# A first router's scores made for both halves ahead of its choice, with two experts' products moved in between

## The reference, cut to what matters

```
def _L1_ffn_ref(x, gate_w, gate_b, w1, w2, w3):        # x: (16, 256, 64), as tokens: 4096 x 64
    logits = einsum('bsd,de->bse', x, gate_w) + gate_b # 16 logits a token
    probs = softmax(logits); top_probs, top_idx = top_k(probs, 2)
    top_probs = top_probs / sum(top_probs)
    dispatch = sum(one_hot(top_idx, 16) * top_probs[..., None], axis=-2)
    h1 = einsum('bsd,edh->bseh', x, w1)                # hidden 128
    h2 = einsum('bsd,edh->bseh', x, w2)
    expert_out = einsum('bseh,eho->bseo', silu(h1) * h2, w3)
    return einsum('bseo,bse->bso', expert_out, dispatch)
t = t + _L1_ffn_ref(_ln_t(t), ...)
```

## Time and profile before

| | us |
|---|---|
| median of 3 runs | 706.9 |
| the three runs | 706.47, 706.9, 711.89 |
| profiled execution, its own time | 704.68 |
| its span | 702.9 |
| TensorE busy in it | 623.2 (89%) |
| VectorE busy | 450.8 (64%) |
| ScalarE busy | 364.4 (52%) |
| GpSimd busy | 260.5 (37%) |

### The profile page before, as it was taken

The page is one execution under the profiler, slowest core; times in us unless marked ns, Lnnn a source line. Parts: engine busy times, 40 slices in busy tenths (PEclk is TensorE's granted clock), DMA queues, the critical chain, the costliest instruction groups (busy, mean ns, idle before and its releaser), DMA issues.

```text
span 702.9 us, 12272 instructions
## 1 busy us (share of the span) xinstructions
PE 623.2 (89%) x3776; PEld 412.3 (59%) x3776; DVE 450.8 (64%) x1323; ACT 364.4 (52%) x777; POOL 260.5 (37%) x349
## 2 busy tenths in 40 slices
PE   7887788886999999999998998998999999996784
PEld 5675437774555555555556776895545445465652
DVE  6555797878777787778776477565433333438566
ACT  3234586176544444444436454455666777435375
POOL 6402555250653543444353000270333333335153
PEclk8999998798999999999999899989999999999897
DMA  4900000204343433524301000022222222100001
GB/s 110 159 6 1 2 0 1 61 2 101 87 112 76 97 83 68 113 61 112 68 9 30 1 2 0 1 51 52 77 70 80 60 61 61 31 2 0 2 2 60
DMA packets 24532, 34.62 MB, mean 49 GB/s; under 512 B 10984, under 2 KB 20224, under 8 KB 22368
## 3 DMA queue, kind: packets, MB, share of 16 engines
q1 hardware_dynamic: 24480, 33.95, 20.8%
HBM read 32.50 MB, written 1.44 MB: 48 GB/s over the span
## 4 chain that ended last, share of the span: by engine, by line
PE 61%; DVE 24%; ACT 6%; issue 4%; POOL 3%; DMA 1%; DVEq 1%; ACTq 0%; SPq 0%; POOLq 0%
PE ps L1808 13%; PE ps L2384 9%; PE ps L2400 8%; PE ps L1828 6%; DVE ST L492 3%; PE ps L2506 2%; PE ps L426 2%; PE ps L784 2%; PE ps L609 1%; PE ps L2782 1%; PE ps L1589 1%; PE ps L2111 1%; PE ps L2089 1%; PE ps L2113 1%; DVE tk L1106 1%
## 5 line engine op out<-in xcount | busy, mean ns | idle before, releaser
L1500 POOL TENSOR_TENSOR out_acc<-out_acc,tok_tmp 128x512 f32<-128x512 f32 x80 | 103.6, 1295 | 211.3 <-DVE tok_tmp L1717 114.7
L1808 PE MATMUL ps<-tokT,w 128*128 128x512 f32 x512 | 134.5, 409 | 3.4 <-DVE hid_buf L1712 1.9
L1769 ACT ACTIVATE act_buf<-ps 128x512 f32<-128x512 f32 x128 | 75.8, 596 | 92.0 <-PE ps L1808 88.4
L1808 PEld LDWEIGHTS ps<-tokT,w 128*128 128x128 f32 x512 | 92.6, 190 | 52.6 <-issue 24.3
L2384 PE MATMUL ps<-tokT,w 128*128 128x512 f32 x256 | 67.7, 406 | 1.5 <-ACT hid_buf L2357 1.5
L2384 PEld LDWEIGHTS ps<-tokT,w 128*128 128x128 f32 x256 | 45.4, 188 | 28.4 <-ACT hid_buf L2357 13.9
L426 PE MATMUL ps<-ones 128*128 128x128 f32 x416 | 58.4, 294 | 1.4 <-DVE X L1005 1.4
L1712 DVE TENSOR_TENSOR hid_buf<-act_buf,ps 128x512 f32<-128x512 f32 x64 | 43.5, 685 | 19.9 <-ACT act_buf L1769 16.3
L426 PEld LDWEIGHTS ps<-ones 128*128 128x128 f32 x416 | 53.6, 206 | 3.9 <-DVE X L1005 1.7
L1712 DVE TENSOR_TENSOR tok_split<-act_buf,ps 128x512 f32<-128x512 f32 x64 | 43.4, 686 | 15.7 <-ACT act_buf L1769 14.7
L537 ACT ACTIVATE U<-X,nmr,rstd 128x64 f32<-128x64 f32 x104 | 36.5, 430 | 23.4 <-POOL nmr L515 18.3
(11 more groups left out here) (475 smaller groups left out, 1133.7 us busy)
## 6 DMA issues: line engine op xcount, KB each, us to landing
disp_all<-disp_dram SPq DMA_DIRECT2D x32, 512.0 KB, 6.1
disp_all<-disp_dram SPq DMA_DIRECT2D x32, 256.0 KB, 3.9
w_raw<-in_L_ffn_w SPq DMA_DIRECT2D x4, 512.0 KB, 7.8
XIN<-in_x SPq DMA_DIRECT2D x4, 256.0 KB, 3.8
w_raw<-in_L_ffn_W SPq DMA_DIRECT2D x2, 512.0 KB, 5.8
out<-XIN SPq DMA_DIRECT2D x4, 256.0 KB, 2.2
fc_raw<-in_L_conv_upfc_w SPq DMA_DIRECT2D x1, 512.0 KB, 4.6
w<-in_L_ffn_w SPq DMA_DIRECT2D x1, 512.0 KB, 11.6
```

Of the source, the lines that this page charges most:

```text
L1500: pool.tensor_tensor(out_acc[:, :], out_acc[:, :], weighed[p % 2], ALU.add).then_inc(mm["acc"].sem, 1)
L1769: act.activation(act_buf[e % 2][:, :], ps[:, e % 2, :], ACT.Silu).then_inc(mm["act"].sem, 1)
L1808: last = pe.matmul(ps[:, 2 * k + e % 2, :], w12[:, part, k, EXPERT1[e], :], tokT[:, bass.ts(i, CHUNK)], start=(part == 0), stop=(part == 1))
```

## The change

Four places move; no instruction is added or taken out, and no tile changes. VectorE makes the logits of both halves first, then five steps of the first half's choice, then the gate products of experts 0 and 1 of chunk 0, then the other six steps. The steps of the second half's choice, one behind each gate product, start at expert 2 in place of expert 0. TensorE makes `hidden(0, 2)` and `hidden(0, 3)` too ahead of the router's transposes of the first half. ScalarE moves their result behind the Silu of expert 3, not of expert 1.

```diff
             router_logits(dve, mm, route1, 0, E1, b_gw[:, :], 6)
+            router_logits(dve, mm, route1, 1, E1, b_gw[:, :], 7)
             for step in range(5):
-                router_top2(dve, mm, route1, 0, E1, step)
-            router_logits(dve, mm, route1, 1, E1, b_gw[:, :], 7)
-            for step in range(5, TOP2_STEPS):
                 router_top2(dve, mm, route1, 0, E1, step)
...
-                    if prev is None:
-                        router_top2(dve, mm, route1, 1, E1, e)
+                    if prev is None and e == 1:
+                        for step in range(5, TOP2_STEPS):
+                            router_top2(dve, mm, route1, 0, E1, step)
+                    if prev is None and e >= 2:
+                        router_top2(dve, mm, route1, 1, E1, e - 2)
...
-                    if prev is None and e == 1:
+                    if prev is None and e == 3:
                         router_move(act, mm, 0, 5)
...
-            router_transpose(pe, mm, route1, 0, (5, 6))
             wwait(pe, "w3")
...
                     if prev is not None or e >= 2:
                         hidden(i, e)
+                    if e == 3 and prev is None:
+                        router_transpose(pe, mm, route1, 0, (5, 6))
```

## The result

| | before | changed |
|---|---|---|
| median | 706.36 us (20 runs) | 711.0 us (20 runs) |
| lowest and highest | 702.05, 711.89 | 707.43, 716.5 |
| ratio | | 1.007, 95% interval 1.0049 to 1.009 |
| span of the profiled execution | 702.9 | 708.4 |
| first logits copy (L1416 on `XIN`) | 152.27 | 153.59 |

The forecast was 2.4. The two profiled spans differ by 5.5 us, and 1.3 of that lies ahead of the changed place, where both programs are the same; of the fourteen executions profiled here the first logits copy started anywhere from 151.1 to 155.4. Behind it the two run alike: to the next stage's first transposes (L609, at 364.38 and 370.07) it is 212.11 and 216.48 us, 4.37 apart.

What follows compares the result with a forecast made beforehand. TensorE was taken to bound once the experts run, its start set by the choice and load. Later load 1.4, clock 1.0 and second-choice steps 0 made 2.4 us: median 706.9 to 709.3 us, range 707.0 to 711.4.

Steps and rivals of the forecast that it cites:

- The chain through the choice and the load sets the time, not the matmuls moved.: Ahead of expert 8: the choice's end plus some 10.6 us of transposes, move, store and load sets TensorE's dense run.
- The swap is free.: VectorE's second-half logits (2.25 us) trade places with five choice steps (2.28 us); its sum up to there is unchanged.
- Two gate products ahead of step 6 put the choice's end off by 1.7 us.: On VectorE, gate products of experts 0 and 1 plus a 0.2 us wait end the first choice 1.7 us later.
- The transposes at full clock give back 0.3.: The first half's router transposes take 0.38 us, not 0.70, so move, store and load shift by 1.4 us.
- The matmuls' gain is swallowed by the load: Ahead of expert 8: TensorE finishes at 174.3, not 175.5; VectorE's wait becomes about 3.8 us, TensorE's stop 3.6.
- The stop costs the clock, 1.0 us.: Behind TensorE's 3.6 us stop, from 177.9, slow work loses 1.0 us, with ends of 0 and 2.6.
- Two more steps of the second choice behind expert 8: nothing, at most 0.3.: Six steps remain in place of four, some 1 us of VectorE, covered by its idle time and TensorE's output products.
- rival C: A long slow stretch: TensorE's clock stays low for twice the work, 4.3 us, 711.2 us; chance 0.12.
- A (the clock holds): TensorE's clock holds over the stop, leaving only the 1.4 us of later load, 708.3 us; chance 0.27.
- B (the load isn't the bound): The load lands sooner or doesn't hold VectorE, so earlier gate products gain 1.0 us, 705.9 us; chance 0.07.
- E (the swap does nothing): Gate products 0 and 1 fall into waits of VectorE, time as before; chance 0.02.
- D, the table load: The Silu's table switch ahead of the two gate products costs 1.4 us more, 710.7 us; chance 0.02.

Runs made afterwards that it cites:

- VectorE's part alone: Changed kernel with VectorE's order kept, but TensorE's eight matmuls and ScalarE's move put back where they were; first logits copy to first output transposes 46.71 us, ratio 1.0064.
- third: Changed kernel with the last six steps of the second half's choice right behind expert 7's gate product, in the load wait; ratio 1.0048.
- sixth: Changed kernel with GpSimd's first three adds of chunk 0 eight columns wide and its first three weight subtractions put off; first logits copy to first output transposes 46.37 us.
- both together with 12 calls: Changed kernel with six steps of the second choice in the load wait and 12 calls of unread matmuls ahead of expert 10; ratio 1.004.
- fourth: Changed kernel with a fill of 20 calls (two matmuls each, result unread) ahead of expert 10 of chunk 0, in TensorE's stop; ratio 1.0087.
- both with 20 calls: Changed kernel with six steps of the second choice in the load wait and 20 calls of unread matmuls ahead of expert 10; ratio 1.0028.
- the kernel with 22 calls: Kernel before with logits swapped, two second-choice steps in VectorE's load wait, and 22 calls of unread matmuls while TensorE waits for the choice; 704.04 us, ratio 0.9959.
- the first two experiments: First: kernel before with only the logits swapped, ratio 1.0012. Second: changed kernel with TensorE's matmuls and ScalarE's move put back, ratio 1.0064.

## Why the prediction came out as it did

The direction held, the mechanism of the tail and the clock held, and 711.0 lies in the range of 707.0 to 711.4; the size was half of what came. By its own steps:

- *The chain through the choice and the load sets the time, not the matmuls moved.* Right: the chain after is the same, and VectorE's part alone makes 3.53 of the 4.39 us.
- *The swap is free.* Right: 43.25 against 43.18.
- *Two gate products ahead of step 6 put the choice's end off by 1.7 us.* Right: 1.64.
- *The transposes at full clock give back 0.3.* Wrong in this execution: 0.70 us. The clock fell at 163.06, 4.1 us after TensorE's last matmul, and not 2.3 us after it as in the trace of before, so the slow stretch reached over the transposes. The eight matmuls, which were to bring the clock back, ran from 161.81 to 164.97 while it fell, and it was back only at 169.9. Of the six kernels with this order up to there, the transposes took 0.70 us in four (changed, third, sixth, and both together with 12 calls) and 0.44 in two (fourth, and both with 20 calls). The term varies from run to run. The load took 6.72 us and not 6.62 besides: tail 1.76 for 1.4.
- *The matmuls' gain is swallowed by the load; VectorE's wait grows to 3.8 us, TensorE's stop to 3.6.* The wait was 3.81. The stop was 3.03, since the experts' matmuls ran slow till 169.9 and gained only 0.2 us, not 1.0.
- *The stop costs the clock, 1.0 us.* Right in kind, 1.31 in size; with the fill the stretch was 1.01 shorter and the output products took 1.94 us in place of 2.58.
- *Two more steps of the second choice behind expert 8: nothing, at most 0.3.* This is **the step that failed**, with 1.29 us. I counted VectorE's time at 0.42 us a step, over the idle 0.46 us. I never asked what GpSimd would be doing at the new place of those steps. The earlier trace rows show VectorE's idle time and nothing of GpSimd. The sign was in the trace of before: the same kind of step, L1450 at 176.43, took 0.58 us beside a GpSimd add and not 0.42, and I read past it. Two lesser slips stand in the same step: the second half's choice ended 7.8 us later on the place's own clock, not 3, and its transposes at 189 stood 9.5 us behind its former end, not eight. They still came 6.1 us behind its new end, so nothing hung on it.

The sum 1.4 + 1.0 + 0 was really 1.76 + 1.31 + 1.29. That 711.0 still lies in the range is luck: its upper end was drawn for rival C, and the room that C needed was filled by the step that had been put at nothing. Rivals: A (the clock holds), B (the load isn't the bound) and E (the swap does nothing) did not come; C's time (711.2) is the nearest to the measured one, by another road, since only one slow stretch of 3.4 us fell behind the stop. Of D, the table load, the trace shows 1.28 us and the Silu right behind it, so no drain was paid.

## What to carry to other kernels

Before work is put ahead of something, ask what hangs on that something: here 1.4 us of gate products went ahead of a chain of transposes, move, store and load of 10.6 us that stayed as long as it was, and gained work for an engine that was waiting for the chain anyway. Free engine time has a place: the same VectorE steps cost nothing inside the wait for the load, up to the end of the stretch, and 1.3 us two experts later beside GpSimd. And when a longer stop of TensorE is the price, count the clock behind it, or fill the stop, with a fill measured in us and not in calls. Here that gain shows in the trace of the place and is too small to show in the whole time. And measure a gain at the end of the stage too: 0.6 to 0.8 us of what the moved steps had gained was lost again behind the place.

## What the runs showed of the hardware

**VectorE and GpSimd in each other's way.** A 128x256 product or sum on VectorE with both inputs in on-chip tiles took 0.42 us alone and 0.54 to 1.15 beside a GpSimd add of 128x512 or subtraction of 128x256 (0.54 in the kernel with 22 calls, 1.15 in the fourth experiment). GpSimd's add took 1.45 and not 1.29 at times, and its subtraction 0.92 and not 0.74. Either one can pay: in the changed kernel L1442, begun at 178.45, kept its 0.42 us, and the add begun 0.09 behind it took 1.45. VectorE's gate and weigh products of 128x512, which have one input in `ps`, took 0.69 us with or without GpSimd. With the adds eight columns wide it was 0.42 again. The Trainium skill (SBUF — State Buffer, "Who interferes with whom") says that a VectorE product of two tensors both in on-chip memory takes a port that GpSimd reads by, as an exclusive lock; the trace agrees: 0.42 against 0.95 us for the one kind, 0.69 for the other.

**The clock's fall isn't at a fixed distance from the last matmul.** In the same place it fell 2.3 us after it in one execution (157.63 to 159.96, before) and 4.1 us after it (158.98 to 163.06, changed), with 1.2 us of new work already done, in another. In the first two experiments it was 3.9 and 4.3 us. The Trainium skill (TensorE: Matmul & The Clock Gate, the part on the clock gate) says that the watch runs freely; the two executions agree with it.
